# Layer norms on POOL: the epsilon's place, and the shape of the normalising instructions

## The reference

```python
def _layernorm(x, axis=-1, eps=1e-05):
    m = jnp.mean(x, axis=axis, keepdims=True)
    v = jnp.var(x, axis=axis, keepdims=True)
    return (x - m) / jnp.sqrt(v + eps)
...
x = x + _L0_xattn_ref(_layernorm(x, axis=-1), ctx_1024, ...)   # layer 0
x = x + _L0_ffn_ref(_layernorm(x, axis=-1), ...)               # 1: soft mixture of 16 experts
x = x + _L1_xattn_ref(_layernorm(x, axis=-1), ctx_1024, ...)   # 2
x = x + _L1_ffn_ref(_layernorm(x, axis=-1), ...)               # 3: 64 routed experts
x = x + _L2_xattn_ref(_layernorm(x, axis=-1), ctx_1024, ...)   # 4
x = x + _L2_ffn_ref(_layernorm(x, axis=-1), ...)               # 5: 8 experts, top 2
x = x + _L3_xattn_ref(ctx_1024, ctx_1024, _layernorm(x, axis=-1), ...)   # 6
x = x + _L3_ffn_ref(_layernorm(x, axis=-1), ...)               # 7: quantised, with a convolution
```

## Time and profile before

| | |
|---|---|
| median of 3 runs | 1001.0 us (999.52 to 1004.35) |
| the profiled execution's own time | 1000.0 us |
| its span, first to last instruction | 998.3 us |
| mean granted TensorE clock | 0.967 of full speed |
| busy: PE, DVE, POOL, ACT | 927.4, 711.0, 575.5, 524.4 us |
| power on POOL (L610), 128x4 | 28 times, 28.2 us |
| subtraction and multiplication on POOL (L617, L618), 128x512 | 13 times each, 13.5 us each |
| the same of layer 7 (L734, L737) | 4 times each, 4.2 us each |
| epsilon on DVE (L1276), 128x4 | 28 times, 8.4 us |

### The profile page before, as it was taken

The page is one execution under the profiler, slowest core; times in us unless marked ns, Lnnn a source line. Parts: engine busy times, 40 slices in busy tenths (PEclk is TensorE's granted clock), DMA queues, the critical chain, the costliest instruction groups (busy, mean ns, idle before and its releaser), DMA issues. The chain is left out here.

```text
span 998.3 us, 16014 instructions
## 1 busy us (share of the span) xinstructions
PE 927.4 (93%) x4685; PEld 719.5 (72%) x4685; DVE 711.0 (71%) x1657; ACT 524.4 (53%) x1028; POOL 575.5 (58%) x564
## 2 busy tenths in 40 slices
PE   8898998898896999999999999999998799989896
PEld 5677675655694856888888888888876776667664
DVE  5776776999454788666666666666657888886865
ACT  3545666454634256666666666666661334443354
POOL 6511544677513156777777777777763449984500
PEclk9999999999997989999999999999999689999898
DMA  6000000222000000000000000000002000000001
GB/s 189 2 1 1 1 1 11 82 68 72 11 1 26 2 9 13 25 25 24 24 24 24 24 24 24 26 24 24 24 1 106 1 1 0 1 1 1 1 11 33
DMA packets 27112, 23.99 MB, mean 24 GB/s; under 512 B 3419, under 2 KB 23987, under 8 KB 26803
## 3 DMA queue, kind: packets, MB, share of 16 engines
q1 hardware_dynamic: 27059, 23.34, 7.8%
HBM read 22.28 MB, written 1.05 MB: 23 GB/s over the span
## 5 line engine op out<-in xcount | busy, mean ns | idle before, releaser
L1796 PE MATMUL psum<-xw 128*128 128x512 f32 x1392 | 366.2, 397 | 3.9 <-DVE xw L1442 2.6
L1796 PEld LDWEIGHTS psum<-xw 128*128 128x128 f32 x1392 | 260.1, 189 | 62.5 <-issue 7.2
L662 POOL TENSOR_TENSOR hh<-arena,hh 128x512 fp32r<-128x512 f32 x176 | 228.2, 1296 | 82.6 <-ACT hh L826 81.2
L1796 PE MATMUL psum<-hh,wdn 128*128 128x512 f32 x672 | 196.5, 396 | 3.6 <-POOL hh L707 2.2
L1604 DVE TENSOR_TENSOR psum<-psum,arena 128x512 f32<-128x512 f32 x176 | 123.1, 700 | 104.1 <-PE psum L1796 97.8
L1069 ACT ACTIVATE arena<-psum 128x512 f32<-128x512 f32 x176 | 105.3, 598 | 120.3 <-PE psum L1796 120.2
L826 ACT ACTIVATE hh<-arena 128x512 fp32r<-128x512 f32 x228 | 142.5, 626 | 46.0 <-DVE arena L1726 42.9
L1796 PEld LDWEIGHTS psum<-hh,wdn 128*128 128x128 f32 x672 | 125.7, 188 | 42.8 <-POOL hh L707 15.1
L1609 DVE TENSOR_TENSOR arena<-psum,arena 128x512 f32<-128x512 f32 x176 | 121.7, 692 | 7.6 <-DVE psum L1604 1.7
L1796 PE MATMUL psum<-arena 128*128 128x18 f32 (+7 forms) x776 | 107.8, 315 | 11.1 <-ACT arena L826 6.5
L610 POOL TENSOR_TENSOR rstd<-veps,neghalf 128x4 f32<-128x4 f32 x28 | 28.2, 1009 | 129.7 <-DVE veps L1276 96.8
(11 more groups left out here) (289 smaller groups left out, 1429.0 us busy)
## 6 DMA issues: line engine op xcount, KB each, us to landing
egu<-in_w SPq DMA_DIRECT2D x44, 128.0 KB, 2.0
egu<-in_egu SPq DMA_DIRECT2D x16, 256.0 KB, 2.5
edn<-in_w SPq DMA_DIRECT2D x44, 64.0 KB, 1.8
edn<-in_edn SPq DMA_DIRECT2D x16, 128.0 KB, 2.0
arena<-in_w SPq DMA_DIRECT2D x1, 1536.0 KB, 6.7
X<-in_x SPq DMA_DIRECT2D x4, 256.0 KB, 4.4
arena<-in_conv SPq DMA_DIRECT2D x1, 1024.0 KB, 8.9
out<-X SPq DMA_DIRECT2D x4, 256.0 KB, 2.3
```

The lines of the kernel that those rows point to most:

```text
L662: pool.tensor_tensor(hh[:, s % 4, 1, :], h1[:, s % 2, :], hh[:, s % 4, 0, :].bitcast(F32), ALU.subtract).then_inc(hh_lo, 1)
L1796: return pe.matmul(dst, lhsT=lhsT, rhs=rhs, start=start, stop=stop)
```

## The change

It has three parts. In every layer but the second (L = 1), the addition of epsilon leaves DVE: `ln_stats` signals ln_var with its last bn_aggr, with no wait behind it, and POOL adds epsilon to the 128x4 variances, waits for that, and takes the power. Where POOL applies the norm, the two 128x512 instructions with a wait between them become four tensor_scalar instructions of 128x128, one per tile, that subtract and multiply with two per-partition scalars, as DVE's L1283 does. In layer 7 `scaled(0)` thereby stands between the power of group 1 and the whole of its normalisation.

```diff
--- before.py
+++ after.py
@@ -607,6 +607,8 @@
             def ln_power(L, g):
                 s = slice(4 * g, 4 * g + 4)
                 pool.wait_ge(ln_var, NG * L + g + 1)
+                if L != 1:
+                    then(pool.tensor_scalar(veps[:, s], mv[:, s, 1], EPS, None, ALU.add))
                 pool.tensor_tensor(rstd[:, s], veps[:, s], neghalf[:, s], ALU.pow).then_inc(ln_rstd, 1)
                 if applied_behind(L, g):
                     pool.wait_ge(ln_rstd, NG * L + g + 1)
@@ -614,8 +616,9 @@
                         pool.wait_ge(ln_xn, NG * L + g)
                     if L == 1:
                         pool.wait_ge(ln_tp, g + 1)
-                    then(pool.tensor_tensor(xn[:, s, :], X[:, s, :], wide(mv[:, s, 0:1], 4, D), ALU.subtract))
-                    pool.tensor_tensor(xn[:, s, :], xn[:, s, :], wide(rstd[:, s].unsqueeze(2), 4, D), ALU.mult).then_inc(ln_xn, 1)
+                    for t in range(4 * g, 4 * g + 4):
+                        last = pool.tensor_scalar(xn[:, t, :], X[:, t, :], mv[:, t, 0:1], rstd[:, t:t + 1], ALU.subtract, ALU.mult)
+                    last.then_inc(ln_xn, 1)
 
             def gate_up0_low(n, k, f):
                 pool.wait_ge(wgu_hi, n + 1)
@@ -1268,12 +1273,12 @@
                 then(last)
                 for t in ts:
                     last = dve.bn_aggr(mv[:, t, :], stats[:, t, :])
-                then(last)
                 s = slice(4 * g, 4 * g + 4)
-                if L == 1:
+                if L != 1:
+                    last.then_inc(ln_var, 1)
+                else:
+                    then(last)
                     dve.tensor_scalar(veps[:, s], mv[:, s, 1], 1.0 + EPS, EPS * EPS, ALU.mult, ALU.add).then_inc(ln_var, 1)
-                else:
-                    dve.tensor_scalar(veps[:, s], mv[:, s, 1], EPS, None, ALU.add).then_inc(ln_var, 1)
 
             def ln_apply(L, g):
                 dve.wait_ge(ln_rstd, NG * L + g + 1)
```

## The result

Before took 1002.67 us (median of 4 runs, 999.52 to 1005.54), after 1019.86 us (4 runs, 1016.52 to 1021.18). The ratio is 1.0164 (95% interval 1.013 to 1.0198): the change costs 1.6%. The forecast was 996.5 us, a gain, with a range of 990 to 1005. Brackets behind a ratio hold its 95% interval from here on. After's profiled execution took 1016.52 us, the shortest of its four; its span is 1014.8 us, 16.5 us longer than that of before.

A forecast was written before the change was run, and what follows sets the result against it. PE was taken to bound the kernel, with POOL and DVE on the path in late norms. +0.3 - 1.4 - 1.6 - 1.6 = -4.3 us from 1000.0 gave 995.7; the median, 1.0 above, 996.7, stated as 996.5, range 990 to 1005.

The forecast's parts named there:

- What bounds the kernel: Whole kernel: PE busy 927.4 of 998.3 us; a norm can cost time only in the some 70 us PE leaves.
- The tensor_scalar: POOL's norms: each new 128x128 tensor_scalar with two per-partition scalars takes t = 0.35 us, bounds 0.20 and 1.0.
- The epsilon: On POOL: each 128x4 epsilon takes 0.20 us plus 0.08 for its wait, 0.28 between two POOL instructions.
- Layers 4 and 6, -0.7 each: Norms into layers 4 and 6: shorter groups on POOL outweigh added epsilons, net -0.7 us each.
- Layer 5, -1.6: Layer 5: the loop of DVE's epsilon and POOL's power shortens from 3.36 to 2.73 us; -1.6 us.
- the slower rival: POOL's norms: four fixed parts and a dear epsilon; with t = 0.8, +12 us, 1013; chance 0.15.
- Layer 7, -1.6: Layer 7: first group ready 0.67 us earlier, `scaled(0)` starts about 1.5 us earlier; -1.6 us.
- the lock: Layers 5 and 7: a running POOL instruction holds DVE's epsilon, 0.98 us for 0.18; moving the epsilon removes this.
- Covered groups at no price: Layers 0 and 1: three POOL groups each run under attention, gain 0.76 and lose 0.28 us at no price.
- Starts and tails, +0.3: Layer 0's start and tails into layers 2 and 3: first group 0.09 us later each time, +0.3 in all.
- The rival of the scalars as a second input: POOL's norms: scalars cost as much as a second input, t = 0.46; -1 us, 1000; chance 0.21.
- The clock did not stay up in layer 5: Rival for layer 5: PE's idle shrinks, its clock stays up, some 2.5 us more gained, 994; chance 0.17.

The follow-up runs named there:

- three_passes: The kernel before, with POOL's 128x512 subtraction in the norms done twice, with the same result; 1016.46 us, ratio 1.0151 [1.0115, 1.0187].
- eps_only: The kernel before, with only the epsilon addition moved from DVE to POOL; 1005.77 us, ratio 1.0037 [1.0011, 1.0063].
- after_busy: The changed kernel with more matmuls that only keep PE busy ahead of layers 4 and 6; 1015.05 us, ratio to before 1.0131 [1.0101, 1.0162].
- reduce_eps: The kernel before, with DVE adding epsilon by a tensor_reduce over variance and epsilon instead of a tensor_scalar; 1002.34 us, ratio 1.0008 [0.9983, 1.0033].
- order7_only: The kernel before, with only layer 7's `scaled(0)` moved in front of group 1's subtraction; 1002.4 us, ratio 1.0011 [0.9987, 1.0034].
- tiles_covered: The kernel before, with the four tensor_scalars per group used only in layers 0 and 1; 1002.96 us, ratio 1.0014 [0.9991, 1.0037].
- tiles_only: The changed kernel with epsilon back on DVE, keeping layer 7's new order; 1011.81 us, ratio to before 1.0097 [1.0068, 1.0126].

## Why the prediction was wrong

**What bounds the kernel: right.** Layers 4, 5, 6 and 7 were named; they grew by 15.8 us, where the profiled span grew by 16.5. That a longer POOL is enough to lengthen them is what three_passes shows. One sentence of that step fails: that a norm can cost time only where PE leaves some 70 us. At the lower clock PE's own work grows too, from 927.4 to 931.7 us with the same 4685 instructions.

**The tensor_scalar: the step that failed.** "I take t = 0.35 us, nearer the one-input row, since what grows with the size is one stream." It is 0.80. The number of streams doesn't set the cost of this form: with one stream it takes 2.49 ns per element for one operation and 3.34 for two, where the old form with its broadcast operand takes 1.67. The cast's 289 ns had no arithmetic in it and wrote bf16; which of the two makes it cheap wasn't tested. The bounds of 0.20 to 1.0 did hold 0.80, and the turning point of 0.5 us was worked out; but t above 0.5 had a chance of only 0.15. That was too little, since no row of before showed a POOL instruction with scalars and arithmetic, and one small arithmetic instruction, the power, took 1.02 us.

**The epsilon: right.** 0.235 us and 0.07 for the wait, 0.31 together, for a forecast of 0.28. It alone costs 0.37% (eps_only), which the working had only as part of its terms: norm 4 grew by 1.1 us for the working's 0.09 + 2 x 0.28 + 0.15 = 0.80. Norm 6 grew by 2.4, with a granted clock of 0.79 and 0.87 from 900 to 910 us, and got 0.9 of it back in the experts ahead of it.

**Layers 4 and 6, -0.7 each: wrong by t.** With t at 0.80 the same sum gives +2.9, the chain shows +2.9 in both, and after_busy's norms +3.2 and +3.6. Beyond it came the clock, which the working didn't have: 1.3 and 1.7 us.

**Layer 5, -1.6: wrong.** The loop did end and DVE's epsilon was no longer in it. But 2.73 us between powers became 4.59, as 0.31 + 1.14 + 3.14 says. The stage gave +3.2; the slower rival had +3.5. reduce_eps adds that the loop's removal was never worth much by itself.

**Layer 7, -1.6: wrong.** `scaled(0)` comes 8.69 us after the first add instead of 8.39: the 0.84 us of the new order (order7_only) went under 1.0 us of tensor_scalars ahead of it and the epsilon. The rounding of group 0 still ended 0.48 us earlier than before, 10.69 us after the first add (942.96) instead of 11.17 (929.45); so what the working looked at was not the loss. The step "Groups 1 to 3 gain more on POOL; PE hides it" was: DVE waits 1.31 us for group 1's tensor_scalars (at 945.48 below), and group 1's scaling starts 17.70 us after the first add (949.97) instead of 15.85 (934.13). The part on the lock was right: the two roundings took 0.43 and 0.47 us (1.25 the first one before). After's timeline:

```profile
940.96 1.04 POOL L731 TENSOR_TENSOR arena<-xn,arena 128x512 f32<-128x512 f32 x1 [0.24 <-DVE arena L1337]
941.98 3.46 POOL L741 TENSOR_SCALAR xn<-X,mv,rstd 128x128 f32<-128x128 f32 x4
942.03 0.43 DVE L1342 TENSOR_SCALAR arena<-arena 128x512 f32<-128x512 f32 x1 [0.19 <-POOL arena L731]
942.49 0.47 DVE L1343 TENSOR_SCALAR arena<-arena 128x512 f32<-128x512 f32 x1
...
945.48 0.69 DVE L1333 TENSOR_REDUCE arena<-xn 128x4 f32<-128x512 f32 x1 [1.31 <-POOL xn L741]
```

**Covered groups at no price: right** (tiles_covered). **Starts and tails, +0.3: open.** The spread of the first stretch, up to 5 us between profiles, hides it.

**The rivals.** The one named slower described what happened: t = 0.8, norms 4 and 6 +2.9 each, layer 5 +3.5, layer 7 +2.5, 1013 us. Measured are 4.5, 5.3, 3.2 and 2.8; the clock makes most of the difference. That its 0.8 us is the measured 0.80 was luck: no row gave it, only the power's 1.02 us beyond it. Its reason was half right: of the 1.0 us that a group pays, all is the fixed part of four instructions, but only because the cost per element, which it didn't name, eats what fusing should have saved; and the epsilon was not dear (0.235 us). The rival of the scalars as a second input had the scalars' cost nearly right (0.145 us for two) and the instruction's wrong. Its -0.6 for layer 5 should be -0.5 by the working's own rule (0.09 - 3 x 0.19), and layer 7's +2.5 and -1.1 stand without a working.

The clock did not stay up in layer 5. By windows of 1 us it fell between 786 and 787 us, some 4 us behind layer 4's add (781.88), and stayed at 0.50 from 790 to 810; in before it fell between 781 and 782, some 6 us behind that add (775.59). And yet PE's wait for DVE's third add had shrunk from 2.13 to 1.10 us (the row at 787.04), as the rival said. That after shows 0.80 from 780 to 790 us where before shows 0.56 is only because its layer 5 comes 6 us later.

## What to carry to other kernels

Before fusing two instructions into one of another kind, find or measure the new form at two sizes; the number of streams it reads did not tell its cost on POOL here, and splitting into tiles pays the fixed part each time. Where no row shows the form at all, give the side beyond the turning point a real chance. And where an engine sets the pace, ask what the lengthened wait does to PE's clock: in two of four stages here it added about a half to the loss that the chain shows.

## What the runs showed of the hardware that was not expected

- On POOL a tensor_scalar is dearer per element than a tensor_tensor with a broadcast operand, even with one immediate: 1488 ns against 1042 ns for 128x512 in fp32. Two operations cost 1922 ns with immediates, 2073 with pointers.
- POOL's tensor_tensor holds a DVE tensor_scalar (0.98 us for 0.17), POOL's tensor_scalar hardly does (0.17 us in its middle, once 0.32), and a DVE tensor_reduce isn't held by the tensor_tensor at all (0.16 us). In after and in tiles_only, where DVE's two roundings (0.43 and 0.47 us) ran beside POOL's tensor_scalars, those took 3.46 and 3.45 us instead of 3.14 and 3.12, so there it seems to have been POOL that gave way.
- A short arithmetic instruction doesn't cost like another of its size: on 128x4, 0.235 us for an addition of an immediate, 0.386 for two operations with two pointers, 1.03 for the power.
